# One order per engine over the whole run in place of lockstep periods, in a two-layer transformer kernel on Trainium2

## The chip, the core and the metric

The kernel runs on one core of one Trainium2 chip. The metric is the device time of one execution in microseconds. An engine is one of TensorE (PE), VectorE (DVE), ScalarE (ACT), GpSimd (POOL) and SyncE (SP, which only issues DMAs). Each works through its own instruction list in order and meets the others at semaphores.

## The reference

Input x has 64 sequences of 128 tokens of width 128; ctx has 64 sequences of 120 tokens. Four residual layers follow each other:

```python
x = x + xattn0(layernorm(x), ctx)      # 16 heads of 8; q and k are RMS-normed per head; softmax; projection
x = x + ffn0(layernorm(x))             # ternary weights, 8 bit activations: 128 -> 512, conv of 3 taps, silu, 512 -> 128
x = x + xattn1(layernorm(x), ctx)      # one head of 128; softmax; fused output projection of [x, attention]
x = x + ffn1(layernorm(x))             # 8 experts, I = 256: silu(x Wg) * (x Wu) Wd, weighted by a softmax gate
```

The inputs are float32. In ffn1 the capacity covers every token (K = S), so each expert sees all tokens and the gather and scatter of the reference drop out.

## The kernel before, in words

**Groups and stages.** The 64 sequences are worked on in 16 groups of 4 (512 token columns). A group passes five stages: **n** (first layer norm, the transposes, q, k, v, the RMS norm of q and k by Newton steps on VectorE, the split of q and k in float16 high and low parts, and their DMA transposes), **a** (the 16-head attention and its projection), **b** (the quantised feed-forward), **d** (the second attention and the gate) and **c** (the eight experts in 16 units u of 128 hidden columns). A short stage **w** prepares the weights.

**Stage a.** Each sequence needs the row maximum of its scores before the exact pass. The approximate scores come from one matmul per four heads of the high parts of q with a block diagonal copy of k, `kbd` (line 568, 128x480 columns, four per sequence, 16 per group). VectorE reduces each to negated maxima (line 1155) and writes them into `q_st`, whose stack is transposed (stacks, line 577, copied by ScalarE in line 813), so that the exact scores (line 591) come with the maximum already subtracted. ScalarE takes the exponential (line 817), TensorE multiplies by the values (line 601), the result is turned (line 608), divided (lines 1161, 1165), turned back (ont), projected (proj, line 622) and added to the residual (x1, line 1173). `kbd` is filled by 32 small DMAs a group on SyncE's queue (line 444): a half holds two sequences, 16 loads, four for each quarter of the heads (`load_kbd`). The first half of a group may be loaded once the first eight maxima of the group before are taken, the second after all 16.

**Stages b, d and c.** b ends with x2 (line 1240), d with x4 in two float16 parts (line 1281) and the gate. Per unit, c has a g matmul group and a u matmul group (three matmuls of 512 columns each, lines 740 to 742), a tanh on ScalarE (line 883), a product on VectorE (line 1307), a scaled copy on ScalarE (line 897), a product on GpSimd (line 962) and a down projection d (line 750, 8 records). Per expert the result is weighted and summed, for five experts on VectorE (line 1320), for three on ScalarE and GpSimd.

**PSUM.** There are eight banks. S0 and S1 hold the scores, but also stage n's q, k, v and all of stage d; BM holds the maxima, the stacks and ont; BO the values, their turn and proj; PB all of stage b; pg, pu and py the experts. The last three groups put every second unit of the experts in S0, BM and BO. `take(bank, ...)` on TensorE waits until the last reader of a bank has finished.

**The order.** `periods` (its call per engine is at the end of each engine's block) runs 20 periods. Period i holds group i's n, group i-1's a, i-2's b, i-3's d and i-4's c. Within a period the string `TURNS[engine][kind]` says for each engine from which stage the next step comes. The kinds "n", "wna", "nab" and "nabd" are the filling of the pipeline, "nabdc" is the steady one (12 times), and four more kinds drain it. No engine waits at a period's end, but no engine's list passes from one period to the next before all steps of the first are listed. A maximum is a step of stage a, at a fixed place between the steps of the sequence before it (`a_steps`):

```python
steps = [("scores", t, 0), ("max", t + 1, 0), ("scores", t, 1), ("values", t, 0), ("max", t + 1, 1),
         ("values", t, 1), ("max", t + 1, 2), ("max", t + 1, 3), ("turn", t), ("stacks", t + 1)]
```

Step sizes are coarse in places: q, k and v are one step (`qkv`), all of a layer norm on GpSimd is one (`normalise`: the roots and four normalising instructions), the two halves of a convolution tap are one (`taps`), the splits of q and k are one (`rms_q`).

**Matmuls that nothing reads.** `UNREAD` lists for the three filling kinds how many matmuls of the identity TensorE issues at which turn into the free bank pg (line 757): 95 in all.

**The start.** SyncE loads the first x, the identity, Wq, ctx and small vectors; ScalarE's queue loads all other weights, the last three being wd, wg and wu (1 MB each), under the semaphore `rest_in` for all up to wd. Stage w stands in period 1. SyncE loads a group's `xin` when the group before is normalised, `xres` when the sum `xres_b` is formed, `ctxt_b` and `ctxn_b` when the second attention has read them.

## Time and profile before

| | |
|---|---|
| median of 3 runs | 1228.7 us (1226.46 to 1229.22) |
| profiled execution, span from first to last instruction | 1219.6 us |
| the profiled execution's own device time | not given; the fastest run shown is 1226.46 us |
| instructions | 27479 |
| TensorE, VectorE, ScalarE, GpSimd busy | 90%, 81%, 68%, 56% of the span |
| DMA | 53.63 MB, mean 44 GB/s, 512 loads of `kbd` |

An engine's busy time is the union of its instructions. Matmuls are pipelined, so a matmul's own duration contains its latency, and several overlap. A wait is the idle time of an engine just before an instruction, put down to what released it last.

### The profile page before, as it was taken

What the parts mean: (1) busy time and instruction counts of PE and PEld (TensorE: products, weight loads), DVE (VectorE), ACT (ScalarE), POOL (GpSimd) and SP (SyncE); (2) the same over time, 40 slices, a digit from 0 to 9 for tenths busy, and PEclk for the clock granted to TensorE, in tenths of its full rate; (3) what the DMA queues carried; (4) which work ended last, traced back from release to release, by engine and by line L of the source; (5) the groups of instructions that cost most, each with busy time, mean ns of one, the idle gap of its engine ahead of it and who ended that gap; (6) DMA issues with size and microseconds to landing.
All of it is one profiled execution on the core that took longest, in us unless ns stands there. A gap on an engine that the chain in (4) does not pass through costs nothing.

```text
span 1219.6 us, 27479 instructions
## 1 busy us (share of the span) xinstructions
PE 1100.5 (90%) x9891; PEld 789.6 (65%) x9891; DVE 984.3 (81%) x2728; ACT 826.6 (68%) x1685; POOL 682.8 (56%) x827
## 2 busy tenths in 40 slices
PE   1677778999999899999999999999999998989998
PEld 1544555766767676767757676767767675767775
DVE  3668787989899898989898898989898897877653
ACT  1255375878768686768778686868778686868655
POOL 3212134566565747566575748475575747375775
PEclk9688898999999999999999999999999999999999
DMA  6120212121312113121212112130212022011000
GB/s 207 30 55 20 55 36 56 35 47 38 62 38 56 36 34 56 35 53 32 62 38 57 36 38 53 35 64 21 62 38 60 22 35 48 22 23 26 18 10 9
DMA packets 151396, 53.63 MB, mean 44 GB/s; under 512 B 116832, under 2 KB 150624, under 8 KB 150880
## 3 DMA queue, kind: packets, MB, share of 16 engines
q1 hardware_dynamic: 149248, 47.82, 17.7%
q10 hardware_dynamic: 2016, 4.08, 0.9%
q8 instruction: 80, 1.31, 0.4%
q14 instruction: 52, 0.43, 0.1%
HBM read 24.73 MB, written 4.19 MB: 24 GB/s over the span
## 4 chain that ended last, share of the span: by engine, by line
PE 72%; DVE 12%; SPq 5%; POOL 4%; issue 2%; ACT 2%; DMA 1%; POOLq 0%; DVEq 0%; ACTq 0%
PE py L750 16%; PE pa L601 5%; SPq L444 4%; PE pa L568 4%; PE pg L740 4%; PE pu L740 3%; PE pg L742 3%; PE pg L741 3%; PE pu L741 3%; PE pu L742 3%; PE pa L591 3%; DVE q_st L1155 2%; PE pa L608 2%; PE pb L648 2%; POOL xn L921 2%
## 5 line engine op out<-in xcount | busy, mean ns | idle before, releaser
L962 POOL TENSOR_TENSOR moe<-moe 128x512 f32<-128x512 f32 x256 | 336.3, 1318 | 293.7 <-ACT moe L897 147.8
L750 PE MATMUL py<-wd_s,moe 128*128 128x128 f32 x1856 | 248.7, 278 | 3.9 <-POOL moe L962 3.7
L750 PEld LDWEIGHTS py<-wd_s,moe 128*128 128x128 f32 x1856 | 231.7, 192 | 21.7 <-issue 7.8
L883 ACT ACTIVATE tg<-pg 128x512 f32<-128x512 f32 x232 | 139.7, 602 | 104.7 <-PE pg L742 104.0
L1155 DVE TENSOR_REDUCE q_st<-pa 128x4 f16<-128x480 f32 x256 | 168.4, 658 | 34.8 <-PE pa L568 33.6
L1307 DVE SCALAR_TENSOR_TENSOR moe<-tg,pg 128x512 f32<-128x512 f32 x232 | 157.3, 678 | 32.1 <-ACT tg L883 30.1
L897 ACT ACTIVATE moe<-pu 128x512 f32<-128x512 f32 x232 | 140.4, 605 | 33.7 <-PE pu L742 31.8
L817 ACT ACTIVATE probs<-pa 120x512 f32<-120x512 f32 x256 | 139.8, 605 | 22.3 <-PE pa L591 22.0
L568 PE MATMUL pa<-kbd,qht 128*128 128x480 f16 x256 | 96.4, 377 | 30.7 <-DVE q_st L1155 26.4
L740 PE MATMUL pg<-x4h,wg_h 128*128 128x512 f16 x232 | 88.6, 382 | 16.4 <-DVE moe L1307 16.4
L921 POOL TENSOR_SCALAR xn<-x,lnm,lnr 128x128 f32<-128x128 f32 x192 | 88.3, 473 | 5.2
L740 PE MATMUL pu<-x4h,wu_h 128*128 128x512 f16 x232 | 88.1, 380 | 0.0
L742 PE MATMUL pu<-x4h,wu_l 128*128 128x512 f16 x232 | 87.9, 379 | 0.0
L742 PE MATMUL pg<-x4h,wg_l 128*128 128x512 f16 x232 | 87.9, 379 | 0.0
L741 PE MATMUL pu<-x4l,wu_h 128*128 128x512 f16 x232 | 87.9, 379 | 0.0
L741 PE MATMUL pg<-x4l,wg_h 128*128 128x512 f16 x232 | 87.9, 379 | 0.0
L601 PE MATMUL pa<-probs,v_st 120*9 120x128 f32 x2048 | 72.5, 281 | 2.2 <-ACT probs L817 0.9
L813 ACT ACTIVATE st_t<-pa 128x512 f16<-128x512 f16 x64 | 38.3, 599 | 51.1 <-PE pa L577 51.0
L568 PEld LDWEIGHTS pa<-kbd,qht 128*128 128x128 f16 x256 | 25.0, 98 | 70.2 <-issue 31.5
L601 PEld LDWEIGHTS pa<-probs,v_st 120*9 120x9 f32 x2048 | 49.4, 92 | 31.2 <-issue 24.8
L918 POOL TENSOR_TENSOR lnr<-lnv,half 128x4 f32<-128x4 f32 x64 | 65.4, 1022 | 0.0
L1320 DVE SCALAR_TENSOR_TENSOR acc<-py,aff,acc 128x128 f32<-128x128 f32 x208 | 58.4, 343 | 7.0 <-PE py L750 6.9
(198 smaller groups left out, 2514.4 us busy)
## 6 DMA issues: line engine op xcount, KB each, us to landing
kbd<-kht SPq DMA_DIRECT2D x512, 3.8 KB
xin<-in_x SPq DMA_DIRECT2D x16, 256.0 KB, 2.8
xres<-in_x SPq DMA_DIRECT2D x16, 256.0 KB, 3.0
out_x<-acc SPq DMA_DIRECT2D x16, 256.0 KB, 3.2
ctxt_a<-in_ctx_t SPq DMA_DIRECT2D x16, 240.0 KB, 2.7
ctxt_b<-in_ctx_t SPq DMA_DIRECT2D x16, 240.0 KB, 2.9
ctxn_b<-in_ctx SPq DMA_DIRECT2D x16, 240.0 KB, 3.6
wd_s<-in_wd ACTq DMA_DIRECT2D x1, 1024.0 KB, 9.5
```

The source lines that it names most:

```text
L568: pe.matmul(pa[:, BM, 0:4 * SC], qht2[:, g % 2, t, :], kbd[:, t, 4 * c:4 * c + 4, :], start=True, stop=True).then_inc(max_ps.sem, 1)
L601: mm = pe.matmul(pa[32 * n:32 * n + HD + 1, BO, i * S:(i + 1) * S], v_st[0:SC, t, HQ * n + i, :], probs[0:SC, i, n, :], start=True, stop=True)
L740: pe.matmul(o[:, :], w_hi[:, us], x4h[:, :], start=True, stop=False)
L741: pe.matmul(o[:, :], w_hi[:, us], x4l[:, :], start=False, stop=False)
L742: pe.matmul(o[:, :], w_lo[:, us], x4h[:, :], start=False, stop=True).then_inc(done.sem, 1)
L750: mm = pe.matmul(moe_y(g, e)[:, j, :], hu[:, u % 3, j * S:(j + 1) * S], wd_s[:, u, :], start=(half == 0 and j == 0), stop=(half == 1), ski ...
L817: act.activation(probs[0:SC, i, :, :], pa[0:SC, i % 2, :], ACT.Exp).then_inc(p_done.sem, 1)
L883: act.activation(tg[:, u % 2, :], moe_bank("g", g, u)[:, :], ACT.Tanh, scale=0.5 / WSCALE).then_inc(tg_done.sem, 1)
L897: act.activation(us[:, u % 3, :], moe_bank("u", g, u)[:, :], ACT.Copy, scale=0.5 / WSCALE ** 2).then_inc(us_done.sem, 1)
L962: pool.tensor_tensor(hu[:, u % 3, :], gw[:, u % 3, :], us[:, u % 3, :], ALU.mult)\
L1155: dve.tensor_reduce(q_st[:, t, 4 * c:4 * c + 4, 3 * HD], pa[:, BM, 0:4 * SC].rearrange("p (h k) -> p h k", h=4), AX.X, ALU.max, negate=Tru ...
L1307: dve.scalar_tensor_tensor(out=gw[:, u % 3, :], in0=tg[:, u % 2, :], scalar=1.0, in1=moe_bank("g", g, u)[:, :], op0=ALU.add, op1=ALU.mult) ...
```

## The change

`periods`, `TURNS` and `run_turns` go. `ORDER` holds one string per engine for the whole run, over seven streams of steps: w, n, m, a, b, d and c. The m stream holds the maxima (16 per group) with their block diagonal loads of the second half; the stacks, scores and values stay in a. `steps_of` lists an engine's steps of a stream for a group, and `run` takes the next step of the stream that the string names, in whichever group that stream stands. In the steady part a row of 108 characters repeats on TensorE: 4 n, 16 m, 22 a, 10 b, 8 d and 48 c.

Steps are split finer: q, k, v apart; on VectorE the RMS norm's and the splits' instructions one by one, and the two convolution halves (`right`, `left`) apart, each waiting for the one before when its turn comes; on GpSimd the layer norm's roots apart from the normalising.

What lockstep had ordered silently is waited for: v of group g waits for the values of g-2, the gate of buffers x4 for the experts of g-2, the copies into `q_st` for the stacks of g-2, q's transpose for the maxima of g-2, the affinities for the side experts of g-2, ScalarE's first side expert for two sums of the group before.

All of w stands at the front: on TensorE before group 0's xn1t, on ScalarE before its first copy, on VectorE from its second step on. On GpSimd `a0:xres` stands between group 0's roots and its normalising, and on SyncE the first step is the xres load of group 1. `UNREAD` is empty: no matmul that nothing reads is left. `SIZES` makes the group sizes a list; all 16 are 4, so no size changes.

SyncE's first steps are, by name: xres(1), xin(1), ctxa(1), kht, qht, **kbd1**, ks, **kbd0** of group 0, then group 1's. In the steady part, around group 12: `c7:out a11:xres m12:kbd1 d9:ctxb n12:ks n12:kbd0 n13:xin b10:hit x4 n13:ctxa n13:kht n13:qht c8:out ...`. TensorE's steady part from the last maximum of group 11 to the first of group 12 reads `m11:max c8:u3 c8:d1 d9:p1t c8:g4 c8:u4 d9:oc c8:d2 d9:fused b10:xit c8:g5 a11:scores c8:u5 c8:d3 b10:fc1 a11:values n13:xn1t c8:g6 a11:turn b10:fc1 a11:stacks n13:q n13:k c8:u6 c8:d4 b10:fc1 d9:xn4t c8:g7 c8:u7 m12:max`, and at the seam of two expert stages `c7:d14 c7:d15 a10:ont c8:g c8:u d9:xn3t a10:proj a11:stacks d9:bf m11:max c8:g1`. VectorE has there `c7:d15 n13:ln1 c8:u n13:ln1_mv a10:proj b10:ln2 m11:max b10:ln2_mv c8:u1`.

Before the first expert step TensorE's list holds 4.75 groups of n, 3.81 of m, 2.77 of a, 1.6 of b and 1 of d (before the change: 4, 3, 3, 2 and 1). VectorE's list between `a0:proj` and b0's last step holds the n of group 3, 22 maxima, most of a1 and all of b0; between that and d0's last it holds 12 maxima, most of n4, three quarters of a2 and b1 up to its first h2t.

The diff, cut to its core:

```diff
-UNREAD = {
...
+UNREAD = {}
+TAIL = 3
...
+STAGES = "wnmabdc"
+ORDER = {
+    "sp": (
+        "annnnmnnnnnnnnnmnnnnannmnbbnnnbbnanmdbbnbnnbnnanmdbbnbnbcnnnanmdbbbbncnnnnamdnbbbbnnnmcadnnnbbbbnnncamdnnnbb",
...
+    "pe": (
+        "wwwnnnnnnnnmmmmaammamamnaanmnmamammamaaammamamaaammamamnammaaaamamnamnaanmmmbmambamambaaambamambaaamambamnab",
...
+        "ccbdccmcdbccamccacmcbamccaacbcamccabmcccmcbamccaaccamccbamccamnamccaccdaadmccdmccmccamccdccdcdbcaccbancabann",
...
-        def periods(eng, body):
-
-            body(0, None, None, None, None)
-            body(1, 0, None, None, None)
-            body(2, 1, 0, None, None)
-            body(3, 2, 1, 0, None)
-            body(4, 3, 2, 1, 0)
-            for i in range(5, NG):
-                body(i, i - 1, i - 2, i - 3, i - 4)
-            body(None, NG - 1, NG - 2, NG - 3, NG - 4)
-            body(None, None, NG - 1, NG - 2, NG - 3)
-            body(None, None, None, NG - 1, NG - 2)
-            body(None, None, None, None, NG - 1)
...
+            if engine == "pe":
+                if stage == "a":
+                    each = [(name, t, c) for t in seqs
+                            for name, c in (("stacks", 0), ("scores", 0), ("scores", 1), ("values", 0), ("turn", 0))]
+                    return each + plain("ont proj")
+                if stage == "b":
+                    return plain("xit") + [("fc1", k, 0) for k in range(KB)] + [("h2t", t, 0) for t in seqs] + plain("fc2")
+                if stage == "m":
...
+        def run(engine, do, between=None):
+
+            todo = {stage: iter([(step, g) for g in (range(NG) if stage != "w" else (0,))
+                                 for step in steps_of(engine, stage, g)]) for stage in STAGES}
+            for at, stage in enumerate("".join(ORDER[engine])):
                 if between is not None:
-                    between(kind, at)
-                step = next(steps[stage])
-                do[stage](step, groups[stage])
+                    between(at)
+                step, g = next(todo[stage])
+                do[stage](*step, g)
...
+                elif name == "qht":
                     sp.wait_ge(q_hi_done.sem, q_hi_done.at(g))
-                    sp.dma_start_transpose(qht2[:, g % 2, :, :], heads(q_hi)).then_inc(qht_in.sem, 16)
+                    if g >= 2:
+                        sp.wait_ge(max_ps.sem, max_ps.at(g - 2, 4 * size(g - 2)))
...
+                elif name == "kbd0":
                     sp.wait_ge(kht_in.sem, kht_in.at(g, 16))
                     if g == 0:
                         sp.wait_ge(kbd_clear.sem, 1)
...
+            def load_part(g, half):
+                part = slice(0, first_half(g)) if half == 0 else slice(first_half(g), size(g))
+                for h in range(H):
+                    rows = slice(h * HD, (h + 1) * HD)
+                    sp.dma_start(kbd[rows, part, h, :], kht[rows, part, 0:SC]).then_inc(kbd_in[half][h // HQ].sem, 16)
+
+            def do_m(name, t, c, g):
+                sp.wait_ge(kht_in.sem, kht_in.at(g, 16))
+                if g == 0:
+                    sp.wait_ge(kbd_clear.sem, 1)
+                if later(g):
+                    sp.wait_ge(max_ps.sem, max_ps.at(g - 1, 4 * size(g - 1)))
+                load_part(g, 1)
+
+            def do_a(name, t, c, g):
...
+                    if g >= 2:
+                        pe.wait_ge(o_ps.sem, o_ps.at(g - 2, size(g - 2)))
...
+                    if g >= 2:
+                        pe.wait_ge(u_ps.sem, u_ps.at(g - 2, NU))
...
+                        if later(g):
+                            act.wait_ge(sum_done.sem, sum_done.at(g - 1, 2))
...
+                    if g >= 2:
+                        pool.wait_ge(st_ps.sem, st_ps.at(g - 2, size(g - 2)))
...
+                    if g >= 2:
+                        dve.wait_ge(side_done.sem, side_done.at(g - 2, len(SIDE)))
...
+                elif name == "right":
                     dve.wait_ge(mid_done.sem, mid_done.at(g, t + 1))
-                    h = pb[:, :].rearrange("p (t s) -> p t s", t=GB)
-                    left, right = cv[:, t % 2, :, 0:S - 1], cv[:, t % 2, :, 1:S]
-                    cb.link(dve.scalar_tensor_tensor(out=right, in0=h[:, :, 0:S - 1], scalar=cw_s[:, t, 0:1],
+                    h, right = pb[:, 0:wide].rearrange("p (t s) -> p t s", t=n), cv[:, t % 2, 0:n, 1:S]
+                    cb.mark(dve.scalar_tensor_tensor(out=right, in0=h[:, :, 0:S - 1], scalar=cw_s[:, t, 0:1],
                                                      in1=right, op0=ALU.mult, op1=ALU.add))
+                elif name == "left":
+                    cb.meet()
+                    h, left = pb[:, 0:wide].rearrange("p (t s) -> p t s", t=n), cv[:, t % 2, 0:n, 0:S - 1]
                     dve.scalar_tensor_tensor(out=left, in0=h[:, :, 1:S], scalar=cw_s[:, t, 2:3],
```

## Rows read from the trace of the kernel before

**Rows 1.** The page: span, and busy time with share of the span.

```profile
span 1219.6 us, 27479 instructions
PE 1100.5 (90%) x9891; PEld 789.6 (65%) x9891; DVE 984.3 (81%) x2728; ACT 826.6 (68%) x1685; POOL 682.8 (56%) x827
```

**Rows 2.** By stretch: start:end and length, busy us (x instructions) of PE, PEld, DVE, ACT, POOL, granted clock, DMA share, GB/s.

```profile
20.00:203.00 183.00, 129.93 (x1216) 95.92 (x1216) 129.10 (x339) 86.05 (x150) 44.59 (x63) 0.87 0.20 45
56.00:89.00 33.00, 23.45 (x278) 15.05 (x279) 20.79 (x38) 18.17 (x28) 2.85 (x2) 0.90 0.21 52
89.00:138.00 49.00, 35.95 (x366) 24.73 (x365) 38.51 (x102) 27.14 (x46) 10.39 (x17) 0.90 0.19 40
138.00:203.00 65.00, 49.86 (x477) 37.32 (x475) 48.79 (x147) 33.77 (x64) 17.92 (x33) 0.92 0.20 43
203.00:1021.00 818.00, 784.02 (x7269) 561.54 (x7269) 721.13 (x2027) 609.07 (x1259) 506.15 (x612) 1.00 0.20 44
1021.00:1219.60 198.60, 186.41 (x1406) 131.99 (x1406) 128.80 (x349) 131.51 (x276) 126.98 (x136) 0.99 0.08 20
```

**Rows 3.** Waits of TensorE between 203 and 1021 us (us in total, times, longest).

```profile
PE pg L740 <- DVE moe L1307: 15.7, 12, 1.3
PE pa L568 <- DVE q_st L1155: 11.7, 12, 1.0
PE pa L577 <- DVE q_st L1155: 3.8, 12, 0.3
```

**Rows 4.** Timeline around the end of a period, VectorE and TensorE.

```profile
608.55 1.13 DVE L1320 SCALAR_TENSOR_TENSOR acc<-py,aff,acc 128x128 f32<-128x128 f32 x4 [0.34 <-PE py L750]
612.22 0.39 PE L740 MATMUL pg<-x4h,wg_h 128*128 128x512 f16 x1 [1.32 <-DVE moe L1307]
614.22 0.36 PE L568 MATMUL pa<-kbd,qht 128*128 128x480 f16 x1 [0.97 <-DVE q_st L1155]
```

**Rows 5.** The chain that ended last (start us, us, what): one matmul, eleven periods apart.

```profile
216.49 1.05 PE pa L691 x2
...
966.32 1.05 PE pa L691 x2
```

**Rows 6.** Source line 1173, the addition that ends stage a (durations in ns, first and last start in us).

```profile
L1173 DVE TENSOR_TENSOR x<-pa,xres_b x16: 678/682/692, 89.3 to 1083.9; 128x512 f32<-128x512 f32 x16
```

**Rows 7.** DMA issues of the first 60 us (the last number is us from issue to landing).

```profile
wd_s<-in_wd ACTq DMA_DIRECT2D x1, 1024.0 KB, 9.5
xres<-in_x SPq DMA_DIRECT2D x1, 256.0 KB, 15.6
```

**Rows 8.** Timeline of the first 60 us: the issues of these two loads.

```profile
6.35 0.46 ACTq L772 DMA_DIRECT2D wd_s<-in_wd  x1
6.80 0.43 SPq L433 DMA_DIRECT2D xres<-in_x  x1
```

**Rows 9.** Timeline of the first 60 us: the loads of group 0, first maximum, first stack.

```profile
37.37 1.61 SPq L466 DMA_TRANSPOSE ks_t<-k_st  x1
39.08 21.27 SPq L444 DMA_DIRECT2D kbd<-kht  x29
46.19 0.37 PE L568 MATMUL pa<-kbd,qht 128*128 128x480 f16 x1
56.55 0.60 ACT L813 ACTIVATE st_t<-pa 128x512 f16<-128x512 f16 x1 [2.27 <-PE pa L577]
```

**Rows 10.** The page's groups: the matmuls that nothing reads.

```profile
L757 PE MATMUL pg<-id_f 128*128 128x128 f32 x190 | 34.5, 313 | 0.0
```

**Rows 11.** Timeline of SyncE in a steady period, and a landing in the chain.

```profile
603.12 11.65 SPq L444 DMA_DIRECT2D kbd<-kht  x16
409.91 1.92 DMA kbd<-kht
```

**Rows 12.** The chain between 590 and 632 us: TensorE's pieces without their latency.

```profile
602.63 0.22 PE pg L741
604.15 0.89 PE py L750 x8
```

More of the change, by code:

```diff
@@ L29 @@
 B, S, SC, D = 64, 128, 120, 128
-GB = 4
-NG = B // GB
+SIZES = 16 * (4,)
+GB = max(SIZES)
+NG = len(SIZES)
+FIRST = tuple(sum(SIZES[:g]) for g in range(NG))
 T = GB * S
@@ L352, in build_program @@
-        n_steps = ["ln1", "xn1t", "qkv", "rms", "rms_k", "rms_q", "qkht"]
-        a_steps = [("max", 0, c) for c in range(4)]
-        a_steps.append(("stacks", 0))
-        for t in range(GB):
-            steps = [("scores", t, 0), ("max", t + 1, 0), ("scores", t, 1), ("values", t, 0), ("max", t + 1, 1),
-                     ("values", t, 1), ("max", t + 1, 2), ("max", t + 1, 3), ("turn", t), ("stacks", t + 1)]
-            a_steps += [step for step in steps if not (step[0] in ("max", "stacks") and step[1] == GB)]
@@ L359, in build_program @@
-        a_steps += ["ont", "proj"]
-        b_steps = ["ln2", "quant", "xit"]
-        for k in range(KB + 1):
-            steps = [("taps", k - 1), ("fc1", k), ("silu", k - 1)]
-            b_steps += [step for step in steps if 0 <= step[1] < KB]
-        b_steps += [(name, t) for t in range(GB) for name in ("h2t", "hit")] + ["fc2"]
-        d_steps = ["ln3", "xn3t", "bf", "s1", "p1n", "p1t", "oc", "fused", "ln4", "xn4t", "gate"]
-        c_steps = []
-        for u in range(NU):
-            c_steps += [("g", u), ("u", u)] + ([("d", u - 2)] if u >= 2 else [])
@@ L690, in do_d @@
                 elif step == "bf":
-                    pe.matmul(pd[:, :], aw1_s[:, :], xn3t[:, :], start=True, stop=True).then_inc(bf_ps.sem, 1)
+                    pe.matmul(pd[:, 0:wide], aw1_s[:, :], xn3t[:, 0:wide], start=True, stop=True).then_inc(bf_ps.sem, 1)
                 elif step == "s1":
-                    for j in range(GB):
+                    for j in seqs:
                         mm = pe.matmul(pd[:, j * SC:(j + 1) * SC], bft[:, j * S:(j + 1) * S], ctxt_b[:, j, :],
@@ L717, in do_d @@
                 elif step == "gate":
-                    for j in range(GB):
+                    for j in seqs:
                         js = slice(j * S, (j + 1) * S)
```

895 lines of the change are left out of this document (463 added, 432 removed).

## The prediction

> **What bounds the kernel now.** I read the page first. TensorE is busy in 1100.5 of 1219.6 us, VectorE in 984.3, the others far less [rows 1]. A share over the whole run hides its stages, so the stretches come next [rows 2]. There the reader should see three regimes. Until 203 us, when the first expert matmul of group 0 is due, no engine is full: of 183 us TensorE shows 129.9 and VectorE 129.1, at a mean granted clock of 0.87. From 203 to 1021 us TensorE works in 784.0 of 818 us, so 34.0 us are lost there; VectorE has 721.1, 88%. After 1021 us, with the expert stage of group 12, the pipeline drains: 186.4 of 198.6 us, 12.2 lost.
>
> Then the waits of TensorE in the middle stretch [rows 3]: 15.7 + 11.7 + 3.8 = 31.2 us of the 34.0, each of them twelve times, each of nearly the same length. So it is one place per period. The timeline shows the place [rows 4]: at 608 us, where one period's list ends and the next begins, the last down projection's combination (1.13 us), stage a's addition, stage b's statistics and the first tanh product stand in a lump on VectorE. TensorE waits 1.32 us for the product that frees bank pg and 0.97 us for a maximum that frees bank BM. Over eleven periods the same matmul is 966.32 - 216.49 = 749.8 us apart, 68.2 us a period [rows 5], of which 784.0/12 = 65.3 are TensorE's work.
>
> **The steady stretch.** The change removes 34.0 us there at most, and nothing below that, as every group still issues the same matmuls. I take the new steady row of orders and walk its seam: after the last down projection TensorE has ont, g, u, xn3t, proj, stacks, bf and one maximum before the next g, 4.3 us (units of three matmuls at 0.22, a down projection 0.89 [rows 12], the rest at the same 0.11 to 0.22 per matmul). VectorE has in that time the combination (1.13), four statistics (about 0.9) and the first product (0.7): done after some 3 us, so pg is free. The maximum before it was taken several steps earlier and is reduced. The seam's three waits therefore go. Elsewhere two g units are never nearer than 1.75 us, against tanh, product and latency of some 1.6: tight, without margin. The convolution's second half no longer follows its first at once, which costs nothing. Of 34.0 us I take 28 as gained and 6 as left in small waits; ends 0 and 34.
>
> **What could replace the seam: SyncE's queue.** The change moves the second half of the block diagonal loads, which belongs to the maxima, ahead of ks and of the first half. SyncE must see the last maximum of group g, then issue 16 loads (11.65 us [rows 11], 0.73 each), two context loads (1), a transpose (1.6 [rows 9]) and four loads (2.9), which land in 1.9 [rows 11]: 19.1 us until the first maximum of g+1 may start. In TensorE's order 9 units (0.65 each), 4 down projections (0.89 each) and some 9.5 us of small steps lie between these two maxima: 18.9 us by bare pieces, 19.7 with the 4% by which a period's busy 65.3 us exceed the sum of its pieces. So the wait is 0, or up to 1 us: it lies in the 6 us left. Behind a waiting maximum stand all of TensorE's steps, experts too. What stands behind the second half's wait on SyncE is ctxb, ks and the first half, of which only the first half is urgent. The wait for the output of the group before stands ahead of it, but that sum is ready several us earlier.
>
> **The ramp: the weights.** The weight steps move from period 1 to the front of TensorE, ScalarE and VectorE. The first statistics must wait for the 1 MB of wd, issued at 6.4 us and landed 9.5 later [rows 7, 8], near 16 us. Worse, GpSimd now adds xres before it normalises group 0, and xres, issued at 6.8, lands 15.6 us later [rows 7, 8], at 22.4: the normalising starts near 23.7 instead of 18.0. VectorE's rounding of the weights and the two splits of the expert weights fall into the same hole, so together I take +5 us, ends +3 and +8, and save that work of VectorE later.
>
> **The ramp: the first loads.** In the kernel before, SyncE issues ks (37.4), then the first half, then the second, 29 loads in 21.3 us from 39.1; the first maximum runs at 46.2 and the first stack's copy at 56.6 [rows 9]. Now the second half (16 x 0.73 = 11.7 us) stands before ks and the first half, where nothing needs it. From the transposes (about 36.6 + 5 = 41.6): 53.3, ks 55, first quarter landed 59.8, last quarter 68.6, first stack about 70. That is 14 us late, the 5 above included. What is hidden in it is group 1's projection work.
>
> **The ramp: from the first stack to the first expert.** Before it took 33, 49 and 65 us: to x1 at 89.3 [rows 6], to x2 at 138, to 203. VectorE was busy 20.8, 38.5 and 48.8 us of them [rows 2], 63, 79 and 75%. By the new order stage a carries the same on VectorE, at the same chain of copies: 33. Stage b carries six maxima more: 42/0.79 = 53. Stage d carries four maxima fewer (2.6), no end of the second b (about 5), and a quarter less of the n and a beside it (4 to 5): 36/0.75 = 48. Sum 134 against 147, -13 us; ends -25 (VectorE denser everywhere) and 0.
>
> **The ramp: the fillers.** 95 matmuls that nothing reads go, 34.5 us of TensorE's busy time, each two records [rows 10]. They stood in idle time, so their work costs nothing; their effect on the clock may. With them the clock was 0.87 over the ramp [rows 2]: mixed between 1.2 and 2.4 GHz. The Trainium skill's "TensorE: Matmul & The Clock Gate" (What's actually happening) says that the throttled state is the default and that activity releases it; by this rule removing them speaks against the change, while a reader of the idle time alone would price them at zero. The rows do not show a ramp without them. The useful busy time is at least 129.9 - 34.5 = 95 us; at a mean clock of 0.75, which I take from the 0.87 and the quarter of activity lost, it grows by 95 x (0.87/0.75 - 1) = 15 us, half of it on the chain that leads to the first expert: +8. Ends 0 and +35 (1.2 GHz throughout).
>
> Ramp in all: 14 - 13 + 8 = +9, the first expert at 212 us.
>
> **The drain.** The same work stands after group 12's first expert. Finer steps can take 3 of 12.2 us; ends -8 and +3.
>
> **Sum.** 1219.6 + 9 - 28 - 3 = 1197.6 us of span. The profiled execution is 9.1 us shorter in span than the 1228.7 median in device time, so 1206.7 us: 1207. About 0.2%, 2.5 us, is what measuring can tell from no change.
>
> **The rivals.**
> 1. *The queue becomes the period's wait* (the other side). If ks and the context loads hold the first half's landing so that the chain of 19.1 us is really 23, each of 12 to 14 periods waits 3 us at its first maximum, and the seam's gain is given back: 1228.7 + 9 - 3 = 1235, slower. It decides from about 2 us of wait per period. For it: a margin of less than 1 us, and loads on one queue. Against: the landing of 1.9 us in a period that had the same loads. 12%.
> 2. *The lump is VectorE's load, not the seam.* VectorE has 60 of 65 us; if the new list only moves the lump, the waits reappear in other places: 1228.7 + 9 - 6 = 1232, between 1222 and 1237. For it: 88% busy in the middle. Against: waits in one place only, twelve times. Here too belongs that the change does not do what it says: a period was never a barrier, only an order. 13%.
> 3. *The ramp costs more*: the first expert at 225 to 238, by the clock and the loads. 1207 + 16 = 1223, up to 1232. 20%.
> 4. *The ramp gains*: first expert at 195, 1190. 7%.
> The forecast's own case, 1197 to 1216: 48%.
>
> The Trainium skill's page "Perfetto Trace Analysis" (Optimization Strategy) advises to interleave regimes whose busiest engine differs. By it the ramp, where no engine is full, would be the place to gain; the count of the orders says otherwise, as before the first expert both hold nearly the same TensorE work (n 4.75 groups against 4, m 3.8 against 3, a 2.8 against 3, b 1.6 against 2).
>
> **How the numbers follow.** Faster: 0.48 + 0.07 + 0.13 of rival 3 + 0.02 of rival 2 = 0.70. Same: 0.03 + 0.03 + 0.01 = 0.07. Slower: 0.11 + 0.08 + 0.04 = 0.23. The range 1190 to 1238 leaves out the best ramp with a perfect middle (1228.7 - 8 - 34 - 8 = 1179) and the half clock together with a poor middle (1228.7 + 35 - 10 = 1254).
>
> **What the profile after would show.** Right: a period of 65.5 to 66.2 us; the waits of TensorE for line 1307's product and the maxima gone from one place and under 1 us per period in all; the first expert near 212, the first stack copied near 70, a clock under 0.85 in the ramp. Wrong: waits of TensorE for the block diagonal loads in every period; a first expert after 235; or a period still at 68 us.

## The result and the profile after

The changed kernel takes 1257.4 us (median of four runs, 1256.5 to 1258.7) against 1229.0 for the kernel before on the same chip: a ratio of 1.023, 95% interval 1.021 to 1.026. It is slower, where the forecast was 1207 us, and outside the range.

The page of the changed kernel, its span and busy times (as [rows 1]), and the first row of its chain by engine:

```profile
span 1255.6 us, 27184 instructions
PE 1102.5 (88%) x9701; PEld 775.8 (62%) x9701; DVE 1041.5 (83%) x2728; ACT 835.0 (67%) x1685; POOL 699.1 (56%) x827
PE 35%; DVE 33%; POOL 10%; ACT 7%; issue 6%; SPq 6%; DMA 2%; POOLq 0%; DVEq 0%
```

TensorE has the work it had, less the unread matmuls. VectorE issues the same 2728 instructions, yet it is busy 1041.5 us, 57 more than in [rows 1]. No instruction was added to VectorE, so some of them must take longer.

The stretches, same columns as [rows 2]: the filling up to 203 us, then seven whole periods (from the first tanh of the fifth group to that of the twelfth) of the changed kernel, and, from the kernel before, the same seven:

```profile
20.00:203.00 183.00, 109.76 (x923) 70.23 (x924) 129.90 (x323) 72.90 (x129) 48.78 (x66) 0.74 0.19 45
504.00:997.00 493.00, 466.60 (x4244) 331.40 (x4243) 446.66 (x1184) 361.16 (x736) 305.30 (x358) 0.99 0.21 43
```

```profile
474.00:951.00 477.00, 457.41 (x4242) 327.57 (x4241) 420.54 (x1184) 355.62 (x735) 295.08 (x358) 1.00 0.20 45
```

A period is 70.4 us (before 68.2), and in it the same 169 VectorE instructions take 63.8 us instead of 60.1.

TensorE's waits between 203 and 1021 us, as [rows 3]:

```profile
PE pg L773 <- DVE moe L1363: 17.5, 32, 1.4
PE pa L597 <- DVE q_st L1202: 7.1, 10, 1.5
PE pb L664 <- DVE xn L1251: 7.1, 11, 1.8
PE py L783 <- DVE acc L1377: 4.9, 8, 1.5
PE pa L597 <- DMA kbd<-kht: 1.3, 3, 0.6
```

The one place per period of [rows 3] is gone; in its stead TensorE waits for VectorE at four lines, unevenly. The block diagonal loads cost it 1.3 us in all: SyncE's queue is not what this kernel waits for. GpSimd's product (line 1000) is in no row: it ends one wait of TensorE in the whole trace, of 0.3 us.

Cut at ScalarE's first tanh of groups 0, 4, 11 and 12, read in the timelines, the spans (us) of the kernels of this study are these; the experiments in the lower rows follow.

| kernel | to the first expert | first 4 periods | next 7 | twelfth | the rest | span |
|---|---|---|---|---|---|---|
| before | 201.5 | 272.5 | 477.3 | 68.0 | 200.3 | 1219.6 |
| old order in the new code | 202.7 | 276.3 | 482.7 | 68.4 | 199.8 | 1229.8 |
| changed | 211.2 | 293.2 | 492.7 | 64.0 | 194.5 | 1255.6 |
| changed, product in four pieces | 212.9 | 296.4 | 491.6 | 65.7 | 200.9 | 1267.5 |
| changed, product cut | 210.9 | 275.9 | 470.9 | 63.7 | 190.3 | 1211.7 |
| before, product cut | 198.2 | 272.7 | 476.3 | 69.4 | 196.9 | 1213.5 |
| changed, VectorE's order alone | 209.7 | 287.6 | 475.8 | 63.1 | 194.8 | 1231.0 |
| changed, unread matmuls | 201.3 | 291.4 | 494.1 | 64.1 | 194.6 | 1245.5 |
| before, no unread matmuls | 214.6 | 280.6 | 481.9 | 67.9 | 199.3 | 1244.3 |
| both repairs | 207.2 | 287.4 | 476.7 | 62.6 | 194.8 | 1228.7 |
| both repairs, joined | 208.4 | 287.4 | 470.1 | 63.6 | 195.5 | 1225.0 |

Of the 36 us of span, 9.7 lie ahead of the first expert, 20.7 in the first four periods, 15.4 in the next seven; 4.0 and 5.8 come back at the end. The medians are only 28.5 us apart. Where a profiled execution has a time of its own, its span is 1.9 to 3.1 us below it, so the profiled execution of the kernel before (span 1219.6) was a fast one, some 7 us under the median. Executions of one kernel differ by such amounts, and the granted clock goes with them: over 21 executions of the kernel before, 1221.0 to 1236.2 us, a clock of the whole run that is higher by 0.01 goes with 6.5 us less on average. The row of the old order in the new code (experiment 4) is a second execution of the old order, and against it the changed kernel's losses are 8.5, 16.9 and 10.0 us. So each row of this table can be off by several us.

**Which instructions grew.** Some of VectorE's groups between 203 and 1021 us (count, then busy us and mean ns of one), first before, then changed:

```profile
L1199 DVE TENSOR_SCALAR xn<-xn,am 128x128 f32<-128x128 f32 x48 | 12.0, 313 | 0.4
L1038 DVE SCALAR_TENSOR_TENSOR rr<-nt,rr 128x128 f32<-128x128 f32 x36 | 10.2, 284 | 0.0
L1137 DVE TENSOR_TENSOR qb<-qb,rr 128x512 f32<-128x512 f32 x12 | 8.2, 682 | 0.0
L1190 DVE TENSOR_SCALAR am<-am 128x4 f32<-128x4 f32 x12 | 2.3, 191 | 0.0
L1223 DVE TENSOR_REDUCE am<-pb 128x1 f32<-128x512 f32 x48 | 32.8, 684 | 4.0 <-PE pb L648 4.0
```

```profile
L1251 DVE TENSOR_SCALAR xn<-xn,am 128x128 f32<-128x128 f32 x48 | 22.8, 535 | 0.0
L1079 DVE SCALAR_TENSOR_TENSOR rr<-nt,rr 128x128 f32<-128x128 f32 x33 | 17.9, 543 | 0.3
L1181 DVE TENSOR_TENSOR qb<-qb,rr 128x512 f32<-128x512 f32 x11 | 14.4, 1314 | 0.0
L1242 DVE TENSOR_SCALAR am<-am 128x4 f32<-128x4 f32 x12 | 15.4, 1284 | 0.0
L1277 DVE TENSOR_REDUCE am<-pb 128x1 f32<-128x512 f32 x48 | 32.8, 683 | 2.0 <-PE pb L680 1.9
```

Four kinds of step that read and write SBUF alone took 1.7 to 6.7 times as long; the one on four elements went from 191 to 1284 ns. Steps that read PSUM kept their length (the reduce above, 684 and 683 ns). So did some that use SBUF alone. The statistics have the same length in the changed kernel, though by their start times 77 of 176 of them begin inside a product (11 of 172 before):

```profile
L1043 DVE BATCH_NORM_STATS2 stats<-x 128x6 f32<-128x128 f32 x144 | 31.2, 279 | 0.4
L1084 DVE BATCH_NORM_STATS2 stats<-x 128x6 f32<-128x128 f32 x144 | 31.1, 279 | 0.6
```

The timeline shows what the step on four elements waits for (start, length, engine):

```profile
372.06 1.28 POOL L1034 TENSOR_TENSOR x2b<-x,a2b_s 128x512 f32<-128x512 f32 x1
372.49 3.33 DVE L1242 TENSOR_SCALAR am<-am 128x4 f32<-128x4 f32 x1
373.30 1.27 POOL L1000 TENSOR_TENSOR moe<-moe 128x512 f32<-128x512 f32 x1
374.52 1.27 POOL L991 TENSOR_TENSOR xres_b<-xres,bp_s 128x512 f32<-128x512 f32 x1
```

VectorE's step of four elements starts 0.43 us into a GpSimd instruction and ends as the third GpSimd instruction in a row ends, at 375.8. The wait is inside the instruction, so no view of waits has it. **Theory A**, then: VectorE's steps of certain kinds that use SBUF alone wait for a GpSimd instruction that is running. The kinds that grew are TENSOR_TENSOR, SCALAR_TENSOR_TENSOR, TENSOR_SCALAR and CAST on more than one column. After 203 us some 420 to 430 of VectorE's steps are of these kinds without PSUM; of them, 4 start inside an expert product with at least 0.2 us of it to go in the kernel before, and 65 in the changed one. The rivals: **B**, the new orders or the code's waits do not fit each other; **C**, the product's own latency is the cost.

### The profile page after: what moved, and what is told of

Read it like the earlier page. It is cut to its first block, busy times and chain, and to the rows that moved or that the text cites. A ratio compares the mean times of both kernels' runs of the same rounds, so it can differ in the third digit from the quotient of the medians.

```text
span 1255.6 us, 27184 instructions
## 1 busy us (share of the span) xinstructions
PE 1102.5 (88%) x9701; PEld 775.8 (62%) x9701; DVE 1041.5 (83%) x2728; ACT 835.0 (67%) x1685; POOL 699.1 (56%) x827
## 4 chain that ended last, share of the span: by engine, by line
PE 35%; DVE 33%; POOL 10%; ACT 7%; issue 6%; SPq 6%; DMA 2%; POOLq 0%; DVEq 0%
PE py L783 5%; DVE q_st L1202 4%; DVE moe L1363 4%; SPq L498 4%; POOL xn L955 4%; PE pa L633 3%; PE pa L597 2%; DVE acc L1377 2%; DVE am L1277 2%; DVE h L1272 2%; PE pg L773 2%; ACT probs L849 2%; POOL moe L1000 2%; PE pg L775 2%; PE pg L774 2%
## 5 line engine op out<-in xcount | busy, mean ns | idle before, releaser
L1000 POOL TENSOR_TENSOR moe<-moe 128x512 f32<-128x512 f32 x256 | 331.5, 1296 | 367.6 <-ACT moe L931 221.3
L783 PEld LDWEIGHTS py<-wd_s,moe 128*128 128x128 f32 x1856 | 237.2, 192 | 29.6 <-DVE acc L1377 7.5
L597 PE MATMUL pa<-kbd,qht 128*128 128x480 f16 x256 | 102.2, 399 | 35.8 <-DVE q_st L1202 18.2
L955 POOL TENSOR_SCALAR xn<-x,lnm,lnr 128x128 f32<-128x128 f32 x192 | 101.1, 539 | 1.5
L633 PE MATMUL pa<-probs,v_st 120*9 120x128 f32 x2048 | 76.2, 293 | 0.7 <-ACT probs L849 0.2
L852 ACT ACTIVATE o_t<-pa 128x512 f32<-128x512 f32 x64 | 38.6, 603 | 42.4 <-PE pa L633 42.4
L873 ACT ACTIVATE hr<-pb,magic,sc 128x512 f32<-128x512 f32 x64 | 49.8, 779 | 24.6 <-DVE sc L1283 24.2
L633 PEld LDWEIGHTS pa<-probs,v_st 120*9 120x9 f32 x2048 | 52.0, 96 | 22.3 <-issue 15.7
```

Of the source, the lines that this page charges most:

```text
L597: pe.matmul(pa[:, BM, 0:4 * SC], qht2[:, g % 2, t, :], kbd[:, t, 4 * c:4 * c + 4, :], start=True, stop=True).then_inc(max_ps.sem, 1)
L633: mm = pe.matmul(pa[32 * n:32 * n + HD + 1, BO, i * S:(i + 1) * S], v_st[0:SC, t, HQ * n + i, :], probs[0:SC, i, n, :], start=True, stop=True)
L783: mm = pe.matmul(moe_y(g, e)[:, j, :], hu[:, u % 3, j * S:(j + 1) * S], wd_s[:, u, :], start=(half == 0 and j == 0), stop=(half == 1), ski ...
L955: ins = pool.tensor_scalar(dst[:, j, :], src[:, j, :], lnm[:, i, j:j + 1], lnr[:, i, j:j + 1], ALU.add, ALU.mult)
L1000: pool.tensor_tensor(hu[:, u % 3, 0:wide], gw[:, u % 3, 0:wide], us[:, u % 3, 0:wide], ALU.mult)\
```

## The experiments

**1 and 2. GpSimd's product cut**, in both kernels:

```diff
-  pool.tensor_tensor(hu[:, u % 3, 0:wide], gw[:, u % 3, 0:wide], us[:, u % 3, 0:wide], ALU.mult)
+  pool.tensor_tensor(hu[:, u % 3, 0:64], gw[:, u % 3, 0:64], us[:, u % 3, 0:64], ALU.mult)
```

> The changed kernel with GpSimd's expert product cut from 512 to 64 columns (the other columns of its result are zeros set once; the expert outputs are wrong by that, every other instruction and every order stays). Theory A, VectorE's instructions on two SBUF operands wait out a running GpSimd instruction: of the 99 us by which VectorE's instructions outlast the shortest of their kind, 63 us lie beside this product and go; VectorE's busy time falls from 1041 to about 980 us, the middle period from 70.5 to about 66 us, and the time from 1257 to 1185 to 1215 us. Rival B, the new orders or waits are themselves badly matched (an engine waits for a step that another has placed late): VectorE's instructions keep their lengths and the time stays above 1240 us. Rival C, the product's own 1.2 us on the way to the down matmul costs the time: then the kernel before gains as much from the same cut as this one.

> The kernel before with the same cut of GpSimd's product to 64 columns (the expert outputs are wrong by that), the control of the run above. Theory A: in the kernel before only 12 us of stretching exist in all, so VectorE's busy time falls by at most 12 us and the time by 0 to 12 us, to 1216 to 1229 us. Rival C (the product's latency is what counts): a fall of 40 us or more here too.

Measured: 1216.7 us for the changed kernel (0.991 of before, interval 0.987 to 0.994), 1219.6 for the kernel before (0.994, 0.992 to 0.996). The same cut gives the one 41 us and the other 9, so neither B nor C, as the expectations put them, holds. A milder C stays possible by these two runs: a product whose latency matters only in the new order. Against it stands that the product ends next to no wait of TensorE in the changed kernel (above). The pages, changed kernel with the cut first:

```profile
PE 1089.4 (90%) x9701; PEld 774.8 (64%) x9701; DVE 980.8 (81%) x2728; ACT 833.4 (69%) x1685; POOL 455.4 (38%) x828
```

```profile
PE 1097.7 (90%) x9891; PEld 788.0 (65%) x9891; DVE 982.4 (81%) x2728; ACT 825.9 (68%) x1685; POOL 440.9 (36%) x828
```

VectorE falls from 1041.5 to 980.8 us in the one and from 984.3 to 982.4 in the other. The 99 and 63 us in the expectation were counted against the shortest instruction of each kind, which takes in ordinary scatter; the 61 us by which VectorE's busy time fell is the firmer number.

With the product cut, TensorE's longest wait in the changed kernel is another one:

```profile
PE pa L597 <- DMA kbd<-kht: 8.6, 9, 2.0
PE pg L773 <- DVE moe L1363: 7.1, 20, 1.1
```

So the block diagonal loads are hidden behind VectorE's delay in the changed kernel, and they become the largest wait once it is gone (11.2 us, 11 times, in experiment 14; 6.0 us, 7 times, in experiment 5).

**3. The product in four pieces** of 128 columns.

> The changed kernel with GpSimd's product in four instructions of 128 columns in place of one of 512; nothing is left out. Theory A: a VectorE instruction now waits for a piece of some 0.35 us at most and not for 1.2 us, so the 63 us beside the product fall to 20 to 30 us and the time to 1220 to 1240 us, although GpSimd is busier than before. Rival B or C: no gain, or a loss of some us, since GpSimd's work grows by three instructions per product.

Measured: 1269.2 us (1.034, 1.031 to 1.038), slower by 12 still. Theory A's forecast here was wrong, and that of rivals B and C, no gain or a loss of some us, was right. The groups of GpSimd between 203 and 1021 us, whole and split:

```profile
L1000 POOL TENSOR_TENSOR moe<-moe 128x512 f32<-128x512 f32 x182 | 237.1, 1303 | 290.0 <-ACT moe L931 183.9 <-DVE moe L1363 106.2
```

```profile
L1002 POOL TENSOR_TENSOR moe<-moe 128x128 f32<-128x128 f32 x724 | 330.1, 487 | 206.1 <-ACT moe L931 137.5 <-DVE moe L1365 68.3
559.06 1.26 POOL L1015 TENSOR_TENSOR acc<-side 128x512 f32<-128x512 f32 x1
559.11 1.76 DVE L1180 TENSOR_TENSOR kb<-kb,gg_s 120x512 f32<-120x512 f32 x1
```

A quarter of the columns takes 487 ns, not 326, so GpSimd is busy 39% longer with the product, and a whole product takes some 1.8 us in place of 1.3. VectorE is in fact held less than in the changed kernel: its page has it busy 1028.3 us, 13 less than 1041.5, though it is still held (the last two rows: a step of 0.69 us takes 1.76 beside another GpSimd instruction). So VectorE's length alone does not explain this run. By the table the seven middle periods are no longer than the changed kernel's (491.6 against 492.7 us), and half of the 12 us lies after group 12's first expert (200.9 against 194.5), where TensorE does wait for the product, 3.2 us in four waits. There its latency counts in part.

**4. The old order in the new code**: `ORDER` holds every engine's order of the kernel before in the new fine steps, `UNREAD` its unread matmuls.

> The changed kernel's code, steps and explicit waits with the order of every engine, and the unread matmuls, of the kernel before. Theory A: the order alone is what puts VectorE's instructions under GpSimd's, so the stretching falls back to some 12 to 20 us and the time to within 1 per cent of the kernel before, 1220 to 1240 us. Rival B' (the code is at fault: separate steps, added waits on VectorE, the later second half of the key loads): it stays over 1245 us. If the lockstep itself had cost what was forecast, it would come out under 1215 us.

Measured: 1229.2 us (1.001, 0.999 to 1.004). The finer steps and the added waits cost nothing and bring nothing, within 0.4%; all of the loss is in the order. This takes the code out of rival B, and it makes the forecast's gain from the seam a matter of order as well.

**5. VectorE's order alone.** One period of it, changed kernel above (the other periods were moved in the same way, not by the same places):

```diff
-cnabmbcdmdcmddbcbmbcbcbddbcdcbbacbbabnnbnbdbcdmdnbbcbdmdbcdmcbmbnbncanannbnbnbcmnnnbmbnbcmnnbcbmbcaacmcbmddmamanncn
+cnabmbcdmndcmddcbbmcbbbcdbdccbdbcbbabanbnnbdcbdndmbbcbdmddbmcbcbnmnbncnnbbanmbncnbbbnmcambbncbmcancnnmacbdmdmmaancn
```

> The changed kernel with the order of VectorE's steps alone rewritten: the same steps, waits and the same orders of the other four engines, but VectorE's two-operand SBUF steps moved, by up to some twelve places, out of the stretches in which GpSimd computes. Theory A (what GpSimd's instructions hold up on VectorE is the loss): the stretching falls from 99 to about 40 us, the middle period from 70.5 to 66 to 67.5 us and the time from 1257 to 1205 to 1225 us. Rival B (the orders of the engines do not fit each other, the stretching is a bystander): moving VectorE's steps away from where the order was planned costs time or gives under 5 us.

Measured: 1232.4 us (1.004, 1.001 to 1.007): 25 of the 28 us are back, by the order of one engine, with the other four as the change left them. VectorE is busy 1007.6 us, and 28 steps of the kinds above start inside a product, counted in the same way, instead of 65. Seven whole periods:

```profile
497.00:973.00 476.00, 459.01 (x4244) 329.83 (x4243) 427.77 (x1182) 360.55 (x736) 307.36 (x360) 1.00 0.21 44
```

VectorE has 61.1 us per period, and the period is 68.0. The time misses the expected 1205 to 1225 us: more stretching is left than was hoped, in am<-am (1203 ns on average in this run) and xn above all. Since its steps also fit TensorE's better or worse after such a move, this run alone would not exclude B; with the first two it agrees.

**6. The orders of all five engines moved.**

> The changed kernel with steps of all five engines moved in the same way, in the middle, in the filling and in the drain. Theory A: about as fast as the kernel in which VectorE's order alone was rewritten, within 10 us, since the other orders were not the trouble: 1200 to 1220 us, which beats the kernel before. Rival B: clearly faster than that one, by over 15 us, since the orders are now matched to each other.

Measured: 1235.1 us (1.006, 1.003 to 1.009), no faster than VectorE's order alone, as A had it; but A's 1200 to 1220 us was missed. The seven periods fell to 67.1 us each, against experiment 5's 68.0, while its first four take 293.1 us against 287.6.

**7. The price of the unread matmuls in the kernel before** (`UNREAD = {}`).

> The kernel before without its unread matmuls, to price the term of the prediction that gave them 8 us: the granted clock of the first 203 us falls from 0.87 to about 0.75 and the first expert starts 3 to 12 us later; the time is 1232 to 1241 us. If the clock of the filling does not lie on the path, the time stays at 1229 us.

Measured: 1243.5 us (1.013, 1.008 to 1.019), 15 us slower, which is past the expected 1232 to 1241.

```profile
20.00:203.00 183.00, 114.00 (x930) 71.95 (x928) 124.42 (x310) 79.95 (x140) 41.29 (x55) 0.65 0.20 42
214.58 0.60 ACT L879 ACTIVATE tg<-pg 128x512 f32<-128x512 f32 x1 [1.90 <-PE pg L738]
```

The granted clock of the filling falls from 0.87 to 0.65, most of it then at 1.2 GHz, and the first expert comes at 214.6 in place of 201.5 us. TensorE is busy 114.0 us of that stretch, at the lower clock, against 129.9. The rest of this profile's 24.7 us lies behind the first expert (table), and the granted clock shows most of it: of its first twelve periods four have a granted clock of 0.98, and these take 70.5 to 71.0 us where most others take 68.0. Two periods next to each other:

```profile
563.20:631.20 68.00, 65.38 (x608) 46.87 (x606) 60.19 (x170) 50.74 (x105) 42.04 (x52) 1.00 0.22 45
631.20:701.90 70.70, 66.81 (x608) 47.15 (x607) 62.13 (x170) 50.73 (x105) 41.85 (x52) 0.98 0.20 43
```

The profile of the kernel before has no such period after 203 us. This profiled execution took 1246.3 us, of four from 1238.7 to 1246.3, and that of the kernel before lies 7 us under its median. So the 15 us of the medians is the price, and these two profiles cannot divide it.

**8. SyncE's order in the filling.**

```diff
-        "annnnmnnnnnnnnnmnnnn
+        "annnnnnmnnnnnnnmnnnn
```

> The changed kernel with one edit in SyncE's order: in the first group the sixteen loads of the second half of the keys stand behind those of the first half and the transposed load of the key stack, and not ahead of both. The first maximum then starts about 11 to 12 us earlier (at 53 in place of 64.6 us). If these loads set the filling, as the prediction had it for the first stack, the first expert comes 5 to 12 us earlier and the time falls by as much, to 1245 to 1252 us; if VectorE's steps set it (in its order the second half is wanted late either way), the time falls by under 3 us.

Measured: 1255.5 us (1.023, 1.018 to 1.029), 2 us less than the changed kernel, which is within the noise, and the first expert is still at 211.2 us.

```profile
55.19 0.37 PE L597 MATMUL pa<-kbd,qht 128*128 128x480 f16 x1
64.95 0.56 PE L597 MATMUL pa<-kbd,qht 128*128 128x480 f16 x1 [9.39 <-DVE q_st L1202]
```

The first maximum's matmul runs at 55.2 (62.9 in the changed kernel), and the second waits 9.4 us for VectorE, whose order has the weight steps there. The loads only hid VectorE's order.

**9 and 10. Unread matmuls put back** into the changed kernel, and into that of experiment 5 (109 of them, `UNREAD = {0: 12, 1: 3, 3: 12, ...}`).

> The changed kernel with 109 unread 128-column matmuls put back into TensorE's waits of the first 200 us, the kernel before having 95 of them; nothing else is touched. If the clock of the filling lies on the path, as in the kernel before, where taking them away cost 15 us, the granted clock from 20 to 203 us rises from 0.74 to 0.85 or more, the first expert starts 4 to 12 us before its 211.2 us, and the time falls to 1244 to 1253 us; the middle period stays at 70.5 us. If VectorE alone sets the filling, the clock rises and the time stays at 1257 us.

> The kernel in which VectorE's order alone was rewritten (1232.4 us), with 109 unread matmuls in TensorE's waits of the first 200 us. Both causes taken together: VectorE's stretching (worth 25 us) and the clock of the filling (worth 4 to 12 us) lie in different stretches, so they add: 1220 to 1229 us. If the filling is VectorE's, it stays at 1232 us.

Measured: 1251.8 us (1.019, 1.012 to 1.026) and 1231.3 us (1.002, 0.998 to 1.006).

```profile
20.00:203.00 183.00, 125.50 (x1174) 91.32 (x1175) 145.35 (x348) 79.45 (x142) 51.78 (x74) 0.88 0.19 46
201.26 0.60 ACT L915 ACTIVATE tg<-pg 128x512 f32<-128x512 f32 x1 [2.15 <-PE pg L775]
```

In the first the clock is 0.88 and the first expert comes 10 us earlier, as in the kernel before; the median gains 5.6 us, but its four executions spread from 1241.1 to 1258.2 us, so the gain is not sure. In the second the median gains 1 us, and the clock of the filling is 0.80 in the profile, whose execution took 1238.0 us, of ten from 1221.2 to 1238.4. Over these ten the time falls as the granted clock of the whole run rises, from 1238.4 us at 0.964 to 1221.2 at 0.979. So the same unread matmuls go with different clocks in different executions. Whether VectorE's order in the filling, which experiment 5 had moved too, plays a part is not shown.

**11. All orders moved further.**

> The changed kernel with the steps of all five engines moved further, VectorE's two-operand SBUF steps and GpSimd's kept apart and TensorE's waits shortened. Theory A: VectorE's time over the usual length of its instructions falls below 2 us a period (5.4 in the changed kernel), TensorE's idle time to 1 us a period (3.9), the middle period to 65.5 to 67 us and the time to 1195 to 1220 us. Rival B (what is left over is the filling, which this run hardly touches): period under 67 but a time over 1225 us.

Measured: 1253.1 us (1.021, 1.018 to 1.025), a clear miss for both A and B.

```profile
507.00:994.00 487.00, 468.53 (x4248) 328.60 (x4246) 424.74 (x1187) 358.79 (x737) 299.48 (x358) 1.00 0.19 44
```

VectorE is at 60.7 us a period, close to the kernel before's 60.1, but the period is 69.6. TensorE is busy 66.9 us in it (65.3 before) for about as many matmuls, at a granted clock of 1.00. The matmuls themselves kept their length (286 ns on average, 285 before). What grew is the number of times TensorE stops: 76 in the seven periods against 29 before and 34 in experiment 6. Matmuls overlap, and each stop ends an overlap, so part of the loss shows as busy time. Its longest waits are spread over VectorE and ScalarE. So this order fits badly in another way than by VectorE's length; which of its moves did it was not found. The changed kernel has 56 such stops and 466.6 us in seven periods against 457.4, so part of its loss looks the same in TensorE's rows, there beside a VectorE that is held.

**12 and 13. Both repairs.** VectorE's order of the changed kernel up to the first expert and of experiment 5 from there on, with the unread matmuls; and the same joined with the orders of experiment 6 from the fifth group on.

> The changed kernel with both repairs and nothing else: the 109 unread matmuls of the filling (first expert at 201.3 us in that run), with VectorE's order of the changed kernel kept up to the first expert; and VectorE's rewritten order from there on (1021.3 us from the first expert to the end of the span in that run). If the two causes are separate, as the theory has it, the pieces add: a span of 201 + 1021 = 1222 us, a time of 1220 to 1228 us, level with the kernel before or up to 0.6 per cent faster. If the filling cannot be repaired by the clock (the gain of that run was chance), the span is 1231 us or more.

> As the kernel with both repairs, and from the fifth group's expert part on the orders in which all five engines' steps were moved (533 us for the eight periods from there in that run, against 539 with VectorE's order alone). By the pieces a span of 201 + 288 + 533 + 194 = 1216 us and a time of 1213 to 1222 us, faster than both kernels. If joining orders that were made apart costs a wait at the joint, it shows there, in the period of the fifth group, and the time is 1222 us or more.

Measured: 1229.5 us (1.002, 1.000 to 1.004) and 1227.3 us (0.999, 0.997 to 1.001). The joined one is level with the kernel before and 30 us under the changed one; no complete kernel of this study is clearly faster than the kernel before. Both miss what was expected of them, 1220 to 1228 and 1213 to 1222 us. From the first expert on the pieces add within 2 us: 1021.5 us for 1021.3, and 1016.6 for 1015. The filling does not: its first expert came at 207 and 208 us, at a clock of 0.81 and 0.82, and not at 201.

**14. The product replaced by a fill** that reads nothing: `pool.memset(hu[:, u % 3, 0:wide], 0.5)`.

> The changed kernel with GpSimd's expert product replaced by a fill of the same 512 columns with a constant, which writes SBUF and reads nothing (so the product is left out, and the expert outputs are wrong by that); waits and orders stay. It tells apart what holds VectorE up. If any running GpSimd instruction does, VectorE's steps beside it are still stretched, by up to the fill's length. If it is GpSimd's reading, as the Trainium skill's SBUF page has it for VectorE instructions with two SBUF inputs, then the two-input steps (root, rr, qb) keep their usual 280, 280 and 680 ns everywhere beside a fill, and only one-input steps (am, xn), which by that page hold both ports in a faster mode, can still wait; the time is that of the cut product, 1210 to 1225 us.

Measured: 1217.8 us (0.992, 0.989 to 0.995). The same lines as above, in the changed kernel with the fill:

```profile
L1250 DVE TENSOR_SCALAR xn<-xn,am 128x128 f32<-128x128 f32 x48 | 13.4, 404 | 0.0
L1180 DVE TENSOR_TENSOR qb<-qb,rr 128x512 f32<-128x512 f32 x11 | 7.5, 685 | 0.0
L1077 DVE SCALAR_TENSOR_TENSOR root<-nt,root 128x128 f32<-128x128 f32 x22 | 6.4, 289 | 0.4
```

Single instructions are plainer than means: eight of the qb steps start inside a fill and take 676 to 681 ns, seven root steps 291 ns, as without any neighbour; 18 of the xn steps start inside one and take 560 ns, against some 280. So here a GpSimd instruction that only writes does not hold a step with two SBUF inputs, and it does hold a TENSOR_SCALAR with a single one. The fill is also shorter than the product (529 ns against 1303), so the time of this run, like that of the cut, does not tell holding from latency; the lengths of the single steps do show the holding.

## Why the prediction was wrong

**The step that failed is the steady stretch.** It said that the change "removes 34.0 us there at most, and nothing below that, as every group still issues the same matmuls", and walked the new order with the durations of the old rows: 1.13, 0.9, 0.7, a tanh-to-product chain of 1.6. Those lengths belong to an order in which next to no SBUF-only step of VectorE meets a GpSimd product. In the new order VectorE's work per period grew from 60.1 to 63.8 us, and the margin named there, 1.75 us against 1.6, "tight, without margin", was gone: TensorE waits 17.5 us, 32 times, for VectorE's product. Measured: from the first expert to group 12's, +32 us in place of -28. Experiments 1, 2, 5 and 14 show the holding and what it costs; that every microsecond of the loss is this they do not show (experiments 3 and 11).

The prediction left out a rule that the Trainium skill states, because the change adds and removes no operation. Its page "SBUF — State Buffer" (Who interferes with whom) says that a VectorE instruction in a two-port mode, or with two SBUF inputs beside a GpSimd instruction that reads SBUF, and a GpSimd instruction exclude each other, and that whichever issues first keeps the shared pair for the whole instruction. The trace agrees: PSUM readers, reduces and statistics keep their length, and steps with two SBUF inputs (qb<-qb,rr 682 to 1314 ns) and TENSOR_SCALAR steps (am<-am 191 to 1284 ns) wait; experiment 14 agrees with the clause about reading.

**The seam itself.** The waits of [rows 3] did go, but little was behind them. With the product cut in both kernels, the new order needs 470.9 us for seven periods and the old one 476.3: 0.8 us a period, some 9 us over twelve, where 28 were forecast. Part of the rest is the wait for the block diagonal loads that takes the seam's place there (8.6 us). Experiment 4 shows that the lockstep code itself cost nothing: explicit waits with the old order change nothing.

**The filling.** First expert at 211.2 us for a forecast of 212, first stack's copy at 73.8 for 70, clock 0.74 for 0.75. The sum came out right partly by luck, since its terms were not: from the first stack's copy to x1 it took 42 us for a forecast of 33 (x1 at 115.8), and from x2 (170.2) to the first expert 41 for 48 and its share of the 8 for the clock. The loads were given 14 us with the weights; moving them (experiment 8) brings 2 us at most and the first expert none, since VectorE's weight steps stand in the same place. The unread matmuls were given 8; experiment 7 shows 15 in the kernel before, and experiment 9 has the first expert 10 us earlier in the one execution profiled. And the sum stopped too soon. The first four periods take 293.2 us where four steady ones take 282: the changed order brings group 0 to its experts with less of the stages behind it done (second group's x2 at 228.4 us against a first expert at 211.2; before, 198.8 against 201.5), and pays behind the first expert. With the product cut the first four periods still exceed four of the seven that follow by 7 us.

**The drain**: -3 forecast, -5.8 measured, and 4 us more gained in the twelfth period.

**From span to time.** The prediction added 9.1 us to its span, the gap between the profiled span and the median. In the runs of this study the gap within one execution is 1.9 to 4.1 us; the rest of the 9.1 belongs to the one execution that was profiled, whose rows are some 7 us better than the median.

**The rivals.** Rival 1 did not happen (1.3 us of waits for the loads), but with the product cut it shows in part (8.6 us). Rival 2 named the right engine, "VectorE's load", and the waits did reappear in other places as it said; what it lacked is that the load itself grows. That its 1232 us is the time of experiment 5 is chance. Rivals 3 and 4 did not happen: the first expert came at 211.2 us. No rival had the load grow, which is why 1257 lay outside all of them. The share given to "slower" had been 0.23.

**Account of the 28 us.** The cut product takes 41 us off the changed kernel and 9 off the kernel before: 32 us are GpSimd's product holding VectorE, or its latency as the new order uses it. Moving VectorE's steps alone, with the product whole, brings 25 back, so most of it is the holding. The filling costs the new order 9.7 us to the first expert in these two profiles; unread matmuls return 5.6 of the median. Against them stand the order's gains: 0.8 us a period, 4 and 5.8 at the end. These overlap and do not sum exactly. Open are why the repairs of the filling did not add (experiments 10, 12, 13), which moves make TensorE stop so often in experiment 11, and how much of the changed kernel's loss is such stops.

## What to carry to other kernels

When an order of work changes, list for each VectorE instruction with two SBUF inputs, and each TENSOR_SCALAR or CAST within SBUF, which GpSimd instructions can now run beside it, before any duration of the old trace is used again. In these profiles such a wait shows only as a longer mean of one and the same line, never as VectorE's idle time: compare means by line first when an engine's busy time changes without new instructions. Judge a filled pipeline by the time at which the fourth or fifth group is through, not by the first. Before a profile's span is compared with another's, look where its execution lies among the times of its kernel.

## What the runs showed of the hardware that was not expected

- A VectorE step on 128x4 elements took 3.33 us, through three GpSimd instructions in a row, while a like one at 516.33 us got in after one (1.05 us). How many GpSimd instructions went ahead of a waiting VectorE step was not the same each time; what decides it is open:

```profile
516.31 1.05 POOL L981 TENSOR_SCALAR k_st<-k_hi 120x1024 f16<-120x1024 f16 x1
516.33 1.05 DVE L1242 TENSOR_SCALAR am<-am 128x4 f32<-128x4 f32 x1
517.33 1.28 POOL L1000 TENSOR_TENSOR moe<-moe 128x512 f32<-128x512 f32 x1
```

- Cutting a GpSimd instruction into four made each 487 ns where a quarter of 1303 is 326, and the kernel 12 us slower.
- 95 matmuls that nothing reads are worth 15 us in the kernel before, by the granted clock of the first 200 us (0.87 against 0.65).
- A steady period can run partly at the lower clock though TensorE is busy 65 of 68 us in the periods around it: 70.7 us at a granted clock of 0.98 against 68.0 at 1.00 (experiment 7). Such periods come in some executions and not in others.
